# Turning expert input rows by DMA and VectorE, adding expert results on GpSimd, and bf16 mask blocks, in a graph-and-expert layer on one Trainium2 core

## The reference

```python
xn = layernorm(x)
x = x + gnn(xn, edges) + mix(xn)          # gnn: two attention layers over src -> dst edges
# each attention layer, with one self loop for every node:
#   e = leaky_relu(s_src[src] + s_dst[dst]); emax = segment_max(e, dst); ee = exp(e - emax[dst])
#   out = segment_sum(ee / segment_sum(ee, dst)[dst] * h[src], dst)
y = layernorm(x)
probs = softmax(y @ router_w); gates, idx = top_k(probs, 2); gates /= gates.sum(-1)
expert_e = (silu(y @ w_gate[e]) * (y @ w_up[e])) @ w_down[e]
routed = sum over the two experts of gates * expert_e
shared = (silu(y @ ws_gate) * (y @ ws_up)) @ ws_down
alpha = sigmoid(y @ sg_w + sg_b)
x = x + alpha * shared + (1 - alpha) * routed
```

## Time and profile before

| | us |
|---|---|
| median of 3 runs (lowest to highest) | 1607.23 (1606.2 to 1609.92) |
| the profiled execution: own time | 1605.74 |
| its span in the trace | 1603.9 |
| TensorE busy | 1536.1 (96%) |
| VectorE busy | 791.6 (49%) |
| GpSimd busy | 369.9 (23%) |
| ScalarE busy | 347.0 (22%) |
| chain that ended last: TensorE | 83% of the span |
| chain that ended last: VectorE | 9% of the span |
| of it the expert products, L816 | 33% of the span |

### The profile page before, as it was taken

How to read it: one execution, slowest core, us unless ns; L and a number is a source line. 1 busy time by engine, 2 the same in 40 slices (tenths; PEclk the granted TensorE clock), 3 DMA queues, 4 the chain that set the end, 5 groups by cost and what they waited for, 6 DMA issues and landing times.

```text
span 1603.9 us, 22049 instructions
## 1 busy us (share of the span) xinstructions
PE 1536.1 (96%) x8432; PEld 1025.1 (64%) x8433; DVE 791.6 (49%) x1503; ACT 347.0 (22%) x525; POOL 369.9 (23%) x422
## 2 busy tenths in 40 slices
PE   5999999999999899999989999999999999999996
PEld 3566676568889899999886555444444444444442
DVE  8655557886668799876987143111111111111111
ACT  3321122112240445640671110100000100000000
POOL 1187855653300000000000047011111111111111
PEclk9999999999999999999899999999999999999998
DMA  9900010000034427114203248834538211613450
GB/s 259 362 2 2 2 62 1 1 1 1 1 81 118 120 56 210 37 20 106 59 1 103 105 113 178 281 117 154 208 103 283 91 49 49 216 45 120 147 202 21
DMA packets 85339, 163.81 MB, mean 102 GB/s; under 512 B 18874, under 2 KB 48816, under 8 KB 85001
## 3 DMA queue, kind: packets, MB, share of 16 engines
q1 hardware_dynamic: 66903, 119.07, 23.4%
q0 software_dynamic: 12096, 23.27, 6.3%
q10 hardware_dynamic: 6258, 20.40, 4.6%
HBM read 127.75 MB, written 37.56 MB: 103 GB/s over the span
## 4 chain that ended last, share of the span: by engine, by line
PE 83%; DVE 9%; issue 2%; DMA 2%; ACT 1%; SPq 0%; DVEq 0%; POOL 0%; ACTq 0%; POOLq 0%
PE bank L816 33%; PE bank L1651 7%; PE bank L1689 6%; PE bank L1553 5%; PE bank L1466 5%; PE bank L1610 5%; PE bank L1438 4%; PE bank L726 2%; DVE arena L2419 2%; PE bank L1491 2%; PE bank L736 2%; PE bank L754 2%; DVE arena L2388 2%; PE bank L1737 1%; PE bank L810 1%
## 5 line engine op out<-in xcount | busy, mean ns | idle before, releaser
L816 PE MATMUL bank<-arena 128*64 128x384 f32 x3312 | 541.3, 488 | 0.6 <-ACT arena L890 0.6
L816 PEld LDWEIGHTS bank<-arena 128*64 128x64 f32 x3312 | 237.4, 137 | 292.8 <-issue 292.0
L1178 DVE SCALAR_TENSOR_TENSOR arena<-bank,arena 64x384 f32<-64x384 f32 x88 | 50.3, 610 | 356.2 <-DMA arena<-out_dram,arena 209.0
L1689 PE MATMUL bank<-arena 125*125 125x198 f32 (+1 forms) x1200 | 192.4, 322 | 10.3 <-DVE arena L2388 10.1
L1689 PEld LDWEIGHTS bank<-arena 125*125 125x125 f32 x1200 | 186.3, 196 | 14.4 <-DVE arena L2388 14.2
L1651 PE MATMUL bank<-arena 128*125 128x192 f32 x960 | 163.5, 328 | 1.1 <-DVE arena L2341 1.1
L1651 PEld LDWEIGHTS bank<-arena 128*125 128x125 f32 x960 | 157.7, 189 | 1.4 <-DVE arena L2341 1.4
L1344 POOL TENSOR_SCALAR arena<-arena 128x125 bf16<-128x125 f16 x186 | 115.3, 622 | 111.4 <-PE bank L1491 107.0
L2228 DVE TENSOR_TENSOR arena<-arena,bank 125x417 f32 x186 | 109.8, 590 | 52.4 <-PE bank L1491 43.3
L1338 POOL DMA_INDIRECT slot_table<-arena x80 | 112.0, 1400 | 93.4 <-issue 93.4
L707 POOL DMA_INDIRECT out_dram<-arena x44 | 40.1, 912 | 296.1 <-DVE arena L1178 296.1
(11 more groups left out here) (307 smaller groups left out, 1591.7 us busy)
## 6 DMA issues: line engine op xcount, KB each, us to landing
arena<-in_L_ffn_w_gate_dram SPq DMA_DIRECT2D x9, 2304.0 KB, 9.1
arena<-in_L_ffn_w_up_dram SPq DMA_DIRECT2D x9, 2304.0 KB, 10.8
arena<-in_L_ffn_w_down_dram SPq DMA_DIRECT2D x9, 2304.0 KB, 9.2
arena<-score_rows ACTq DMA_DIRECT2D x18, 585.9 KB
expert_in<-arena SPq DMA_DIRECT2D x23, 384.0 KB, 10.5
arena<-expert_in ACTq DMA_DIRECT2D x23, 384.0 KB, 3.5
arena<-in_L_mix_w_qkv_dram SPq DMA_DIRECT2D x2, 2304.0 KB, 17.6
xn_columns<-arena SPq DMA_DIRECT2D x1, 3750.0 KB, 14.8
```

Of the source, the lines that this page charges most:

```text
L816: ins = tp.matmul(ps[bank][HP * h:HP * h + HP, 0:384], frm[:, b, k, HP * h:HP * h + HP], ew[h][i][:, k, n * 384:(n + 1) * 384], start=(k = ...
L1689: ins = tp.matmul(ps[bank][0:T, c * width:(c + 1) * width], ptile[0:T, j % NPT, dt * T:(dt + 1) * T], values(n - first, st), start=(st == ...
```

## The change

The input rows of tiles 1 to 22 are no longer turned by TensorE. ScalarE loads a tile with four transfers, each of which puts a column block of 192 features on 32 partitions (512 pieces of 768 bytes for a tile), and VectorE turns it in blocks of 32x32 with one instruction (`turn_x`). For this the features are dealt to the partitions in another order, six neighbouring ones to each, so gate and up weights are now loaded with six neighbouring rows to a partition, 18432 bytes in one piece. Tile 0 is still turned by TensorE, with a stride, and the loads of tiles 0 and 1 are issued before the seventh of the ten shared blocks. The hidden rows are now turned inside the products: the first half before the last three of the six steps of the last up bank, the second half after the first step of the down products.

VectorE no longer waits for the gathered output rows. It writes the gated result to a buffer, `ybuf` (`take_y`), after a wait that GpSimd has added what the buffer held one tile ago, and GpSimd adds the buffer to the gathered rows.

In the mask stage ScalarE writes the counts as bf16 and TensorE turns them by a bf16 product with a bf16 identity, which VectorE copies once, much earlier. The blocks are 128 columns wide, of which three hold neighbouring values that nobody reads. Some semaphores are merged to keep to their number.

```diff
@@ mask stage
+        countb = words(SMALL + ZB, NTB3 * N, BF16).rearrange("p (b n) -> p b n", b=NTB3)
-                    ins = tp.transpose(ps[(st % 2) * 3 + dt // 4][0:T, (dt % 4) * T:(dt % 4 + 1) * T],
-                                       tbuf[0:T, st % 2, dt * T:(dt + 1) * T], ident[0:T, 0:T])
+                    ins = tp.matmul(ps[(st % 2) * 3 + dt // 4][:, (dt % 4) * T:(dt % 4 + 1) * T],
+                                    countb[0:T, st % 2, dt * T:dt * T + P], ident_b[0:T, 0:T], start=True, stop=True)
-                sc.activation(tbuf[0:T, st % 2], counts[0:T, st, 0:N], ACT.Copy).then_inc(s_cf, 1)
+                sc.activation(countb[0:T, st % 2, 0:NW], counts_all[0:T, st * CW:st * CW + NW], ACT.Copy).then_inc(s_cf, 1)
@@ SyncE: weights
+        ROWS_OF = ("(p k) n -> p k n", "(p k) n -> p k n", "(k p) n -> p k n")
-                sp.dma_start(ew[b][i], w[(NE - 1) * b].rearrange("(k p) n -> p k n", p=P)).then_inc(s_ew[i], 16)
+                sp.dma_start(ew[b][i], w[(NE - 1) * b].rearrange(ROWS_OF[i], p=P)).then_inc(s_ew[i], 16)
@@ GpSimd, for each half of a tile
                     pool.wait_ge(s_yd, 2 * (2 * j + h + 1))
                     pool.wait_ge(s_accin, 16 * (2 * j + h + 1))
+                    pl.tensor_tensor(accb[0:HP, h], accb[0:HP, h], ybuf[0:HP, h], ALU.add).then_inc(s_yadd, 1)
+                    pool.wait_ge(s_yadd, 2 * j + h + 1)
                     pl.indirect_dma_start(out[:, :], ids, accb[0:HP, h], None, bounds_check=N - 1, oob_is_err=False)\
@@ TensorE, tile
-                pe.wait_ge(s_xTs, 2 * j + 2)
+                if isinstance(j, int) and j == 0:
+                    pe.wait_ge(s_xTs, 2)
+                else:
+                    pe.wait_ge(s_xTd, j)
                 for m in range(2):
                     pe.wait_ge(s_ew[m], loads)
                     for i in range(2):
                         for k in range(KD):
+                            if (m, i, k) == (1, 1, 3):
+                                h_transposes(j, b, 0)
                             ins = product(2 * m + i, xgT, b, k, m, i)
-                h_transposes(j, b, 0)
-                if not (isinstance(j, int) and j == NTM - 1):
-                    x_transposes(j + 1, 1 - b)
-                else:
+                if isinstance(j, int) and j == NTM - 1:
...
-                h_transposes(j, b, 1)
...
                     if k == 0:
                         pe.wait_ge(s_hTa, j + 1)
+                    if k == 1:
+                        h_transposes(j, b, 1)
@@ ScalarE
+            def load_x(j, b):
+                rows = xg_dram[bass.ds(j * P, P)].rearrange("(i r) d -> r i d", r=32)
+                for c in range(4):
+                    act.dma_start(xgb[32 * c:32 * c + 32, b].rearrange("p (i d) -> p i d", i=4), rows[:, :, FW * c:FW * c + FW])\
+                        .then_inc(s_xg[b], 16)
             for t in range(NT):
+                if t == 6:
+                    act.wait_ge(s_rows, 16 * 2 * NT)
+                    load_first_x()
+                    load_x(1, 1)
...
-            act.wait_ge(s_rows, 16 * 2 * NT)
-            load_x(0, 0)
-            load_x(1, 1)
-            take_x(0, 0)
+            take_first_x()
@@ VectorE
-            def add_rows(j, h):
-                if h == 0:
-                    dve.wait_ge(s_y, j + 2)
-                dve.wait_ge(s_accin, 16 * (2 * j + h + 1))
...
+            def take_y(j):
+                dve.wait_ge(s_y, j + 2)
+                for h in range(2):
+                    if j:
+                        dve.wait_ge(s_yadd, 2 * (j - 1) + h + 1)
+                    for o in range(2):
+                        dv.tensor_scalar(ybuf[0:HP, h, o * 384:(o + 1) * 384], ps[4 + o][HP * h:HP * h + HP, 0:384],
+                                         slot_info[0:HP, j, h, 0:1], None, ALU.mult).then_inc(s_yd, 1)
+            def turn_x(j):
+                b = j % 2
+                dve.wait_ge(s_xg[b], 64 * (j // 2 + 1))
+                dv.transpose(xgT[:, b].rearrange("p k n -> p (k n)").rearrange("p (k i c) -> p k i c", k=KD, i=4),
+                             xgb[:, b].rearrange("p (i c k) -> p k i c", i=4, k=KD)).then_inc(s_xTd, 1)
+            turn_x(1)
             for j in range(NTM - 1):
                 take_h(j)
                 take_hT(j)
+                if j + 2 < NTM:
+                    turn_x(j + 2)
...
+                    dve.wait_ge(s_fout, 32 * NT)
-                add_rows(j, 0)
-                add_rows(j, 1)
+                take_y(j)
@@ VectorE, much earlier
+            dv.tensor_copy(ident_b, ident).then_inc(s_kvx, 1)
```

More of the change, by code:

```diff
@@ L143, in gps_layer @@
         token_info = small(4 * NT).rearrange("p (k t c) -> p k t c", k=2, t=NT)
+        ident_b = small(P, BF16)
         u1col = small(NQ)
@@ L258, in gps_layer @@
         CW16 = NT * CW // 2 + 1
-        counts_flat = words(SMALL + COUNTS, CW16, U16)[:, 0:NT * CW]
+        counts_all = words(SMALL + COUNTS, CW16, U16)
+        counts_flat = counts_all[:, 0:NT * CW]
         counts = counts_flat.rearrange("p (t n) -> p t n", t=NT)
@@ L271, in gps_layer @@
         tbuf = take(NTB3 * N).rearrange("p (b n) -> p b n", b=NTB3)
+        NW = (NT - 1) * T + P
+        assert (NT - 1) * CW + NW <= 2 * CW16
+        countb = words(SMALL + ZB, NTB3 * N, BF16).rearrange("p (b n) -> p b n", b=NTB3)
         abbuf = take(4 * N).rearrange("p (b s n) -> p b s n", b=2, s=2)
@@ L323, in gps_layer @@
         accb = words(SMALL + V12 + NT * D + KD * N + KD * HG, 2 * D).rearrange("p (b n) -> p b n", b=2)
+        assert 4 * EWW + 2 * D <= V12 + NT * D
+        ybuf = words(SMALL + 4 * EWW, 2 * D).rearrange("p (b n) -> p b n", b=2)
         route = region(P - SMALL, D + GW)
@@ L454, in gps_layer @@
         s_acc = sem("chunk_counted")
-        s_cf = sem("counts_as_float")
+        s_cf = sem("counts_as_bf16")
         s_mskT = sem("mask_psum")
@@ L570, in gps_layer @@
         s_xTs = sem("slot_xT_sb")
+        s_xTd = sem("slot_xT_turned_dve")
         s_h = sem("h_ready")
@@ L573, in gps_layer @@
         s_hTs = sem("hT_copied_dve")
-        s_yd = sem("y_added")
+        s_yd = sem("y_taken")
+        s_yadd = sem("y_added")
         s_last = sem("last_step")
@@ L794, in ffn_pe, with first_x_transposes @@
             pe.wait_ge(s_sout, 2 * NT)
-            def x_transposes(j, b):
-                wait_use(pe, s_xg[b], j, b, 16)
+            def first_x_transposes():
+                pe.wait_ge(s_xg[0], 64)
                 for i in range(2):
                     for k in range(3):
-                        ins = tp.transpose(ps[6 + i][:, k * P:(k + 1) * P], xgb[:, b, (3 * i + k) * P:(3 * i + k + 1) * P], ident)
-                        if isinstance(j, int) and j == 0 and 3 * i + k < 4 and k < 2 and (i, k) != (1, 1):
+                        ins = tp.transpose(ps[6 + i][:, k * P:(k + 1) * P], xgb[:, 0, 3 * i + k:D:KD], ident)
+                        if 3 * i + k < 4 and k < 2 and (i, k) != (1, 1):
                             ins.then_inc((s_g, s_up, s_y)[2 * i + k], 1)
@@ L849, in ffn_pe @@
             pe.wait_ge(s_et, 2)
-            x_transposes(0, 0)
+            first_x_transposes()
             over_tiles(pe, tile)
@@ L877, in ffn_act, with load_first_x @@
             sc.activation(alpha[0:T], lg[0:T, :, NE], ACT.Sigmoid, bias=sgb[0:T]).then_inc(s_exout, 1)
+            def load_first_x():
+                for i in range(4):
+                    act.dma_start(xgb[32 * i:32 * i + 32, 0], xg_dram[32 * i:32 * i + 32]).then_inc(s_xg[0], 16)
+            def load_x(j, b):
[3 more added lines that the diff above has]
+                        .then_inc(s_xg[b], 16)
             for t in range(NT):
+                if t == 6:
+                    act.wait_ge(s_rows, 16 * 2 * NT)
+                    load_first_x()
+                    load_x(1, 1)
                 act.wait_ge(s_shT, t + 1)
@@ L895, in tile @@
                 if not (isinstance(j, int) and j + 2 >= NTM):
+                    if not (isinstance(j, int) and j == 0):
+                        act.wait_ge(s_xTd, j)
                     load_x(j + 2, b)
@@ L901, in tile @@
                 sc.activation(hT[:, b, 0:3].rearrange("p k n -> p (k n)"), ps[0][:, 0:384], ACT.Copy).then_inc(s_hTa, 1)
-                if not last:
-                    take_x(j + 1, 1 - b)
-                else:
+                if last:
                     act.wait_ge(s_h, 2 * j)
@@ L1170, in take_hT @@
                 dv.tensor_copy(hT[:, j % 2, 3:6].rearrange("p k n -> p (k n)"), ps[1][:, 0:384]).then_inc(s_hTs, 1)
-            def add_rows(j, h):
-                if h == 0:
-                    dve.wait_ge(s_y, j + 2)
-                dve.wait_ge(s_accin, 16 * (2 * j + h + 1))
-                for o in range(2):
-                    cols = accb[0:HP, h, o * 384:(o + 1) * 384]
-                    stt(out=cols, in0=ps[4 + o][HP * h:HP * h + HP, 0:384], scalar=slot_info[0:HP, j, h, 0:1], in1=cols,
```

(8 more changed lines are left out.)

29 lines of the change are left out of this document (13 added, 16 removed).

## The result

The changed kernel takes 1594.31 us, the median of four runs (1593.18 to 1598.5), against 1606.72 for the kernel before, four runs (1602.97 to 1609.92). The ratio is 0.9934, with a 95% interval from 0.9915 to 0.9952: 12.4 us faster by the medians, 10.6 (7.7 to 13.7) by the ratio. The forecast was 1586.4, or 20.8 less. So 8 us are missing by the medians and 10 by the ratio, and what follows asks mainly where they went.

What follows compares the result with a forecast made beforehand. TensorE, busy for 96% of the span, was taken as the bound. Tiles 7.9, entry 3.85, VectorE's wait 4.5 and mask 4.6, less 0.1 for the identity copy, make 20.8: 1607.23 - 20.8 = 1586.4, range 1578 to 1597.

Steps and rivals of the forecast that it cites:

- two losses: Range 1578 to 1597 allowed two rival losses at once, such as the eaten mask gain and the remaining VectorE wait.
- unpriced clock: Range allowed up to 2 us either way for the clock falling in stretches not priced.
- the prediction's rivals: Free product changes 1580 (0.10), mask gain eaten 1591 (0.15), VectorE wait remaining 1591 (0.08), GpSimd as pace, slower (0.05).
- Tiles, 7.9: Expert part: input turns leave TensorE, a tile falls from 24.84 to 24.48; 22 tiles give 7.9 us.
- The rival in which changes are free: Expert part: changing product kind costs nothing more, tile drops by the full 0.66, 6.6 us more: 1580; chance 0.10.
- VectorE's wait, 4.5: Expert part, disturbed middle tile: VectorE no longer waits for late output rows, only GpSimd does; 4.5 us gained.
- Mask stage, 4.6: Mask stage: bf16 turns pass once, ten take 0.59 instead of 1.09; 4.0 from eight steps plus 0.6 at the third.
- Entry, 3.85: Entry to expert part: input rows requested earlier, start 2.05 us earlier plus 1.8 of clock gained; together 3.85.
- -2.05: Entry: with rows requested early the start hangs on VectorE alone, 2.05 us earlier.
- the 1.8 of clock: Entry: first 96 rows of products took 17.39 instead of 15.6 at a lowered clock; 1.8 counted as gained.
- the 19.7 of the forecast: Expert part: GpSimd needs 19.7 us per tile, two halves with two additions of 1.9, against TensorE's 24.48.

Runs made afterwards that it cites:

- e10: Changed kernel with two lone 128x128 turns per tile added among the gate products, into a bank nobody reads: 1613.12 us, one run.
- e8: Changed kernel with a second GpSimd addition of the same size for each of 44 halves: 1635.14 us, ratio 1.0170.
- e5: The changed kernel itself run once more, on a second chip: 1596.73 us, ratio 0.9939.
- e3: The kernel before with only the bf16 mask blocks of the change: 1602.88 us, ratio 0.9976.
- e4: The kernel before with only GpSimd's addition and the buffer for expert results: 1601.32 us, ratio 0.9967.
- e1: Changed kernel, but SyncE, not ScalarE, waits for the scattered rows and requests tiles 0 and 1's first input rows, ahead of weights: 1594.27 us, ratio 0.9916.
- e6: e1 with two buffers: odd tiles use the other 64 partitions, so VectorE waits for additions of two tiles before: 1596.49 us, ratio 0.9940.
- e7: e6 with the stores of row blocks 2 and 3 moved behind tile 0's last three expert weights on SyncE: 1591.95 us, ratio 0.9906.
- e9: e7 with all ten row-block stores put behind the landing of tile 0's down weights: 1595.95 us, ratio 0.9910.
- e11: e9 with one buffer for expert results, as in the changed kernel: 1593.64 us, ratio 0.9898.
- e12: e11 loading only 384 of 2304 KB of the second half's first down weight, so the result is not the layer's: 1586.00 us, ratio 0.9871.
- e2: e1's first input-row requests put back behind ScalarE's last shared copy, where they stood before the change: 1596.17 us, ratio 0.9930.

## Why the prediction was right and wrong

The time lies in the stated range, which left room for two losses and for an unpriced clock. But none of the prediction's rivals describes what happened: three of the four terms came as forecast, and the fourth was lost in a place where no loss was named.

*Tiles, 7.9.* Right: 24.48, and e10 shows the 0.15 of each change by a second way. The rule of the Trainium skill (TensorEngine Tiling (Array Packing), Key Properties) that a change of tiling mode drains the engine agrees with both. The rival in which changes are free is excluded. VectorE's turn took 1.58, above the 1.4 that I gave as its upper bound, and is hidden all the same. Weights with long pieces stopped nothing behind the first tile.

*VectorE's wait, 4.5.* Right: in the traces of the change and its variants but e8 such a stop takes at most 0.7 (e5), in the kernels without it (before, e3) 2.9, and e4 alone gives 5.5 (2.7 to 7.9). GpSimd's addition took 1.81, where I took 1.9; the estimate from the Trainium skill (GPSIMD Engine Reference, Elementwise — side-by-side cycle accounting) was 1.7. GpSimd's undisturbed tile is near the 19.7 of the forecast (23.5 of e8 less two second additions of 1.81 is 19.9). Its room is smaller than I gave it.

*Mask stage, 4.6.* Right: the stage is 4.60 shorter, 0.62 of it up to the third turns and 3.98 from there. By e3 the kernel gains 3.9 (1.9 to 5.8). How much reaches the shared expert differs by execution: in the eleven other traces with this stage GpSimd's last scatter is issued 2.5 to 7.3 earlier than in that of before, and in e4's, without it, 1.8 later; against this spread the changed kernel's 2.7 says little.

*Entry, 3.85.* This failed, and it is where the missing time went. The step was: "7 us after GpSimd has issued its last scatter, so ScalarE should not stall the shared blocks". Issue is not landing. The landing takes 20 us and more, and the earlier trace rows shows only the issue. The row that would have told it was on SyncE's timeline of before, its gate weights at 986.57, released by the same semaphore. In place of -2.05 the shared blocks end 8.6 later than before (1014.72 against 1006.15), and the 1.8 of clock that the first tile did gain was paid ahead of it: twelve rows took 7.03, 3.2 more than at full speed.

Behind it stood a second limit that I did not look for. I had asked only whether TensorE would wait for rows. An entry by my numbers starts the first product near 1003.8 (1010.43 less 4.6 and 2.05) and needs the down weights 16.3 later (in e1 the wait begins at 1021.2, after a start at 1004.87), near 1020, but they land at 1023.7 to 1025.4 in e1, e3, e6, e7, e9 and e11, and later still in e4. In the trace of before TensorE needed them only where the chain has

```profile
1029.29 23.37 PE bank L816 x144
```

so they cost nothing there. Measured as what is gained on the kernel before, by the ratios, the changed kernel has 10 to 11 us. e1, which takes away the first limit alone, has 13.5; e11, with the second still there and the stores moved, 16.4; e12, which takes the second away as well, 20.7 (17.0 to 24.3), the forecast's 20.8. The two ends are clear of each other, the steps between are not. No run takes away the second limit alone. The traces say that it would not pay: with the first product at 1017.08 the down weights are wanted near 1033, and nothing waited for them. A stop costs more than itself, too: after the waits of 4.3 to 5.1 in e6, e7, e9 and e11 the clock is at half speed for a while; after e1's wait of 2.5 it is not. In e11 the next pieces take 2.83, 0.83 and 20.58 where 1.51, 0.48 and 20.15 are usual, 2.1 more.

Open: why single executions of one kernel differ by 3 (e12) to 11 us (e6: 1592.0 to 1603.4). Traces show half-clock stretches in other places each time and other landing times, but only one execution per kernel is traced. Because of it, differences of 2 to 4 us between e1, e2, e5, e6, e7 and e9 are weakly held, and the two fastest of the kernels that compute the whole, e7 and e11, can't be told apart. By its ratio e11 takes some 6 us less than the changed kernel; its interval lies clear of e5's (0.9925 to 0.9954) and just overlaps that of the changed kernel's first runs (0.9915 to 0.9952).

## What to carry to other kernels

A wait for a transfer is over when it lands: look for another engine that waits for the same semaphore, and read there when it was let go. Before counting an earlier start as gained, list everything that the started work needs, each with its landing time, since a floor that was hidden by the old delay becomes the bound. Small interruptions that change between column-half and full-array products have a price of their own, 0.15 us for each change here, which can be read from two groups of different length.

## What was not expected of the hardware

- An indirect scatter of 125 rows of 3 KB, the last of twenty issued 1.49 us apart, landed 20 to 29 us after its issue in ten traces and 32 in e4 (16.9 to 18.7 in e9, e11 and e12, which hold the first two stores back).
- The four weights of 2304 KB, with what ran beside them, kept all DMA engines busy (share 0.98 in e11, 1.02 in e7, from 990 to 1020, at 296 and 327 GB/s), and the last came at 1024.6 to 1025.4 whether it was requested at 1002 (e3) or at 987 (e11), but at 1016.5 with 1920 KB less (e12).
- VectorE's turn of 128x768 float32 in 32x32 blocks, read with a stride of six words, took 1.58 us, 2.3 times L919's operation of the same size.
